# One count matrix less: a graph convolution that reads four typed planes in place of their sum

## The chip, the core and the metric

The kernel runs on one core of a Trainium2 chip. TensorE multiplies, VectorE (DVE) and ScalarE (ACT) do elementwise work, GpSimd (POOL) does elementwise work and indirect transfers, SyncE (SP) issues the other transfers. The metric is the device time of one execution in microseconds (us); lower is better. The kernel before took 18697.45 us, the median of three runs (18695.46 to 18709.6).

## The reference, cut to what matters

Four graph layers over 6250 nodes of 64 features and 206250 edges sorted by destination: attention, a graph convolution, message passing with two small networks, and four steps of a gated graph network. Two of them sum neighbours in a way that depends on the edge only through its two ends and its type:

```python
# layer 2, the convolution: the type of an edge plays no part
h = feat * norm[:, None]
agg = jax.ops.segment_sum(h[src], dst, num_segments=n)
rst = (agg @ weight) * norm[:, None] + bias
...
# layer 4, four times: each edge type has its own weights
transformed = jnp.einsum('nd,khd->knh', feat, W) + b[:, None, :]
msgs = transformed[etypes, src]
a = jax.ops.segment_sum(msgs, dst, num_segments=num_nodes)
```

## The kernel before, in words

Nodes stand in 49 blocks (`NB`) of 128 partitions. Both sums above are dense products with a matrix of edge counts: a row for each source node, a column for each destination, the entry the number of edges. The kernel makes these matrices first, in DRAM, and streams them later in chunks.

**The build** (about 302 to 5313 us). Columns are made in pairs, 3248 of them (`VW`; two destinations each, the last 112 for overflow), over 4859 steps (`BSTEPS`). In a step DVE makes two one-hot tiles (`hots_of`, L1690 and L1691, 128x128 and 128x392 elements, f16) in a ring of 8; TensorE multiplies them into a PSUM bank (`count`, L1090) and clears one column of the next bank (L1092). 392 is 2 destinations by 4 types by 49 source blocks. Before every fourth step TensorE loads twelve table values into registers (`fours`). ACT moves finished banks to `stagebuf` (`evict`, L823). When 16 pairs, 32 destinations, are staged, that is one event, 203 in all (`NEV`). For each event:

- SP (`keep`) waits for the evictions, loads four table values, stores the two halves of the four typed planes (L608, 784 KB each) to `adj4`;
- POOL (`untyped`) adds the four planes of the event in three additions of 128x1568 f16 elements (L766, L767, L769) into `ubuf`, a ring of 3;
- SP waits for the sum (`untyped_made`) and stores it to `adj1` (L612, 448 KB). Only then, and once the stores of the event before have landed (L615), does it count that event before as done (`events_done`, L616). ACT waits for this count before it reuses a stage buffer. Of these there are four, and two for the last seven events, which hold the overflow columns (`OBUFS`).

When all stores have landed, SP raises `built` and DVE starts the attention layer (L1697).

**The convolution** (about 8697 to 8948 us). The 6250 destinations are cut in 13 groups: one of 128 columns with 224 overflow columns (352 together), and twelve of 512. The 49 source blocks of `adj1` come in four chunks (`UCH`) of 14 blocks, of which the fourth is half empty: 52 transfers through a ring of four (`DRING`). For each source block TensorE makes two products with the same count columns: one with the first two bf16 parts of the features (L1176, 128 rows of output) and one with the third (L1181, 64 rows, left and right half of the array in turn). After a group come the overflow's share (`conv_fold`), the copy to SBUF by ACT and the product with the layer's weights (`conv_post`).

**The last layer**, four times, does the same with `adj4`: 196 blocks of a group in 14 chunks (L1373, L1378), and a product with the weights after each type.

All orders are written out by hand, one instruction stream per engine; a wait is on a semaphore.

Of the kernel before, what the change touches and what calls it, by code (L numbers as in the profile page):

```python
# [6 lines left out]
P = 128  # L7
N = 6250
D = 64
# [8 lines left out]
KT = 4  # L18
# [45 lines left out]
UCH = 4  # L64
# [5 lines left out]
ULEN = UCH * RUN  # L70
USED = NB * BLK
UBUFS = 3
# [9 lines left out]
ROWS1 = P * UCH * GRP  # L82
# [5 lines left out]
USED0 = NGRP * UCH  # L88
LOADED0 = 16 * USED0 // DRING
# [4 lines left out]
assert BW % GRP == 0 and COMBS % CCH == 0 and BC % 2 == 0 and NB <= UCH * CCH and (NGRP - 1) * 512 + P == NPAD  # L94
# [53 lines left out]
def build(nc, a, out):  # L148
    ctx = ExitStack()
    with ctx:  # L150
# [6 lines left out]
        def dram(name, shape, dt=F32):  # L157
            return nc.dram_tensor(name, shape, dt).ap()
# [10 lines left out]
        event_rows = dram("event_rows", (8, P), I32)  # L169
        adj4 = [dram(f"adj4_{h}", (NGRP * ROWS4 + GRP, RUN), F16) for h in range(2)]  # L170
        adj1 = dram("adj1", (NGRP * ROWS1 + GRP, RUN), F16)
# [72 lines left out]
        ubuf = here("ubuf", [P, UBUFS, ULEN], F16)  # L244
        uhalf = here("uhalf", [P, USED], F16)
# [117 lines left out]
        halves_made, untyped_made = sem("halves_made"), sem("untyped_made")  # L363
# [172 lines left out]
        def _(sp):  # L536
# [58 lines left out]
            table(2, event_rows, 4, eventtab)  # L595
            sp.wait_ge(tab_loaded, 16 * 10)

            def keep(k, j, it):
                last = sp.value_load(eventtab[0:1, k:k + 1] if known(k) else eventtab[0:1, bass.ds(k, 1)], min_val=1, max_val=1 << 14)
                src = sp.value_load(eventtab[32:33, k:k + 1] if known(k) else eventtab[32:33, bass.ds(k, 1)],  # L600
                                    min_val=0, max_val=(SBUFS + OBUFS - 1) * SLEN)
                row4 = sp.value_load(eventtab[64:65, k:k + 1] if known(k) else eventtab[64:65, bass.ds(k, 1)],
                                     min_val=0, max_val=(NGRP - 1) * ROWS4 + GRP - 1)
                row1 = sp.value_load(eventtab[96:97, k:k + 1] if known(k) else eventtab[96:97, bass.ds(k, 1)],
                                     min_val=0, max_val=(NGRP - 1) * ROWS1 + GRP - 1)
                sp.wait_ge(evicted, last)
                for h in range(2):
                    sp.dma_start(adj4[h][bass.ds(row4, ROWS4), :].rearrange("(p c k) e -> p c k e", p=P, k=GRP)[:, :, 0, :],  # L608
                                 stagebuf[:, bass.ds(src, SLEN)].rearrange("p (h c e) -> p h c e", h=2, e=RUN)[:, h, :, :])\
                        .then_inc(stored[j % 2], 16)  # L610
                sp.wait_ge(untyped_made, k + 1)
                sp.dma_start(adj1[bass.ds(row1, ROWS1), :].rearrange("(p c k) e -> p c k e", p=P, k=GRP)[:, :, 0, :],  # L612
                             ubuf[:, j % UBUFS, :].rearrange("p (c e) -> p c e", e=RUN)).then_inc(stored[j % 2], 16)
                if not (known(k) and k < 1):
                    sp.wait_ge(stored[(j - 1) % 2], (it * 3 + (j - 1) // 2 + 1) * 48)  # L615
                    sp.sem_inc(events_done, 1)  # L616
            pipeline(sp, NEV, 6, 0, lambda it, j: stage(NEV, 6, it, j, 0, keep))
            sp.wait_ge(stored[(NEV - 1) % 2], ((NEV - 1) // 2 + 1) * 48)
# [9 lines left out]
            for i in range(NGRP * UCH):  # L628
                n, c = divmod(i, UCH)
                width = GRP if n else GCOLS // BLK  # L630
                if i >= DRING:
                    sp.wait_ge(used, i - DRING + 1)
                sp.dma_start(chunk1[:, i % DRING, 0:width * RUN],
                             adj1[0:NGRP * ROWS1, :].rearrange("(g p c k) e -> g p c (k e)", p=P, c=UCH, k=GRP)[ORDER[n], :, c, 0:width * RUN])\
                    .then_inc(loaded[i % DRING], 16)
# [35 lines left out]
            with sp.Fori(0, LAYERS) as layer:  # L671
                for i in range(GCH):
                    n, c = divmod(i, NCH)
                    width = GRP if n else GCOLS // BLK
                    sp.wait_ge(used, layer * GCH + (max(i - DRING + 1, 0) + USED0))
                    sp.dma_start(chunk4[:, i % DRING, 0:width * RUN],
                                 adj4[c // HCH][0:NGRP * ROWS4, :].rearrange("(g p c k) e -> g p c (k e)", p=P, c=HCH, k=GRP)
                                 [ORDER[n], :, c % HCH, 0:width * RUN])\
                        .then_inc(loaded[i % DRING], 16)
                    if c == 6:  # L680
                        cols = 512 if n else P
                        sp.dma_start(counts[:, n % 2, 0:cols], count_rows[:, ORDER[n] * 512:ORDER[n] * 512 + cols])\
                            .then_inc(count_in[n % 2], 16)
# [8 lines left out]
        def _(pool):  # L692
# [59 lines left out]
            pool.wait_ge(tab_loaded, 16 * 10)  # L752

            def untyped(k, j, it):
                last = pool.value_load(eventtab[0:1, k:k + 1] if known(k) else eventtab[0:1, bass.ds(k, 1)],
                                       min_val=1, max_val=1 << 14)
                src = pool.value_load(eventtab[32:33, k:k + 1] if known(k) else eventtab[32:33, bass.ds(k, 1)],
                                      min_val=0, max_val=(SBUFS + OBUFS - 1) * SLEN)
                pool.wait_ge(evicted, last)
                if not (known(k) and k < UBUFS):  # L760
                    pool.wait_ge(events_done, k - UBUFS + 1 + EPRE)
                if not (known(k) and k < 1):
                    pool.wait_ge(untyped_made, k)
                kinds = stagebuf[:, bass.ds(src, SLEN)].rearrange("p (t e) -> p t e", t=KT)
                to = ubuf[:, j % UBUFS, 0:USED]
                nc.gpsimd.tensor_tensor(to, kinds[:, 0, :], kinds[:, 1, :], ALU.add).then_inc(halves_made, 1)  # L766
                nc.gpsimd.tensor_tensor(uhalf[:, :], kinds[:, 2, :], kinds[:, 3, :], ALU.add).then_inc(halves_made, 1)  # L767
                pool.wait_ge(halves_made, k * 2 + 2)
                nc.gpsimd.tensor_tensor(to, to, uhalf[:, :], ALU.add).then_inc(untyped_made, 1)  # L769
            pipeline(pool, NEV, UBUFS, 0, lambda it, j: stage(NEV, UBUFS, it, j, 0, untyped))  # L770


# [21 lines left out]
        def _(act):  # L794
# [11 lines left out]
            act.wait_ge(tab_loaded, 16 * 10)  # L806
# [54 lines left out]
            act.wait_ge(used, UCH)  # L861
# [67 lines left out]
            with act.Fori(0, LAYERS) as layer:  # L929
                gb, sb4 = layer * NGRP, layer * (NGRP * KT)  # L930

                def sweep(n, k):
                    i = n * KT + k
                    act.wait_ge(used, layer * GCH + (n * NCH + (3, 6, 10, 13)[k] + 1 + USED0))
                    if i >= 2:
                        act.wait_ge(posted, sb4 + NGRP + i - 1)
                    cols = 512 if n else GCOLS
                    nc.scalar.activation(summed4[:, k % 2, 0:cols], bank[k % 2][:, 0:cols], ACT.Copy).then_inc(copied, 1)
# [48 lines left out]
        def _(pe):  # L987
# [71 lines left out]
            turn_table(2, 8)  # L1059
# [13 lines left out]
            pe.wait_ge(tab_loaded, 16 * 10)  # L1073
# [92 lines left out]
            for n in range(NGRP):  # L1166
                cols = 512 if n else GCOLS
                for c in range(UCH):
                    i = n * UCH + c
# [3 lines left out]
                    combs = min(CCH, NB - c * CCH)  # L1173
                    for m in range(combs):
                        hi = c * CCH + m
                        nc.tensor.matmul(bank[n % 2][:, 0:cols], feat1[:, hi, 0:2, :].rearrange("p a d -> p (a d)"),  # L1176
                                         columns(chunk1, i % DRING, m, cols), start=hi == 0, stop=False, skip_group_check=True)
                    for m in range(combs):
                        hi = c * CCH + m
                        half = hi % 2 * D  # L1180
                        last = nc.tensor.matmul(bank[n % 2][half:half + D, 0:cols], feat1[:, hi, 2, :],  # L1181
                                                columns(chunk1, i % DRING, m, cols), start=False, stop=False, skip_group_check=True)
# [124 lines left out]
            with pe.Fori(0, LAYERS) as layer:  # L1307
# [55 lines left out]
                for n in range(NGRP):  # L1363
                    cols = 512 if n else GCOLS
                    for c in range(NCH):
                        i = n * NCH + c
                        times = GCH // DRING + (i % DRING < GCH % DRING)
                        pe.wait_ge(loaded[i % DRING], layer * (16 * times) + (16 * (i // DRING + 1) + LOADED0))
# [52 lines left out]
        def _(v):  # L1421
# [243 lines left out]
            link(both_(out=tabcols[:, 4:6], in0=i2[:, E2], scalar=float(ROWS4), in1=i3[:, E2], op0=ALU.mult, op1=ALU.add))  # L1665
            both_(out=tabcols[:, 6:8], in0=i2[:, E2], scalar=float(ROWS1), in1=i3[:, E2], op0=ALU.mult, op1=ALU.add)\
# [6 lines left out]
            copy_(tabi[0:8, :], bank[7][0:8, 0:P]).then_inc(tab_copied, 1)  # L1673
# [11 lines left out]
            link(nc.vector.memset(ubuf[:, :, USED:ULEN], 0.0))  # L1685
# [406 lines left out]
```

## Time and profile before

| | us |
|---|---|
| median of 3 runs | 18697.45 |
| the profiled execution | 18688.54 |
| its span, first to last instruction | 18686.8 |
| build of the count matrices | 302 to 5313 |
| convolution's products | 8702 to 8948 |

The span is what the trace covers; the execution's own time is 1.7 us more. In the rows below, PE is TensorE's matmuls and PEld its weight loads, which overlap them. Times are us from the start of the span. Behind an arrow in brackets stands what ended an idle time, "issue" being time in which the engine waited for nothing that the profile shows. PEclk is the granted TensorE clock as a share of 2.4 GHz; it takes the values 0.5 (1.2 GHz) and 1.0 (2.4 GHz), and a mean over a stretch lies between them.

### The profile page before, as it was taken

How to read it: one execution, taken by the hardware profiler on the slowest of the kernel's cores; microseconds unless marked ns; L12 is line 12 of the kernel's file. 1: busy time of each engine (PE TensorE's matmuls, PEld its weight loads, DVE VectorE, ACT ScalarE, POOL GpSimd, SP SyncE). 2: the span in 40 equal slices, each digit the busy share in tenths (PEclk: the TensorE clock that was granted, in tenths of full speed). 3: DMA queues.
4: the chain of work that ended last, by engine and by line, in shares of the span. 5: the costliest groups of instructions: out<-in, count | busy, mean ns of one | idle time of the engine just before them, and what ended most of it. 6: DMA issues, size and time to landing. Idle time of an engine off the chain costs nothing.

```text
span 18686.8 us, 316361 instructions
## 1 busy us (share of the span) xinstructions
PE 12122.4 (65%) x67022; PEld 7612.2 (41%) x67023; DVE 7552.7 (40%) x26048; ACT 3559.3 (19%) x9727; POOL 8136.1 (44%) x6693
## 2 busy tenths in 40 slices
PE   3444444444435555556777777677776899999999
PEld 2222222222234444444555555555555544444443
DVE  6777777777743333333333333333333200000000
ACT  1333333333310000000122222222222100000000
POOL 3333333333345555551588888888887000000000
PEclk6555555555555555556899999999999699999999
DMA  2222222222221111114333333333334598989898
GB/s 100 84 84 84 82 82 85 83 84 84 84 60 35 35 35 35 35 35 164 79 41 41 41 41 41 42 41 41 41 41 38 157 342 334 341 331 342 328 345 311
DMA packets 1285108, 2208.14 MB, mean 118 GB/s; under 512 B 407567, under 2 KB 1127717, under 8 KB 1183861
## 3 DMA queue, kind: packets, MB, share of 16 engines
q1 hardware_dynamic: 935388, 1916.06, 29.3%
q0 software_dynamic: 348960, 284.02, 11.5%
q14 instruction: 536, 4.39, 0.1%
q8 instruction: 224, 3.67, 0.1%
HBM read 1647.55 MB, written 551.99 MB: 118 GB/s over the span
## 4 chain that ended last, share of the span: by engine, by line
PE 30%; issue 20%; POOL 13%; another core or an unknown queue 4%; DVE 2%; DMA 1%; DVEq 0%; SPq 0%; POOLq 0%; ACT 0%; ACTq 0%
PE ps L1373 12%; POOL G L469 7%; PE ps L1378 6%; POOL reverse L788 5%; PE ps L1128 3%; PE ps L1118 2%; PE ps L1108 1%; PE ps L1315 1%; POOL scatter_hold L787 1%; DMA reverse<-SD,sidx 1%; PE ps L1176 1%; PE ps L1181 0%; PE ps L1331 0%; PE ps L413 0%
## 5 line engine op out<-in xcount | busy, mean ns | idle before, releaser
L1090 PE MATMUL ps<-hots 128*128 128x392 f16 x4859 | 2210.5, 505 | 2779.9 <-issue 1348.8
L788 POOL DMA_INDIRECT reverse<-SD,sidx x1660 | 2649.2, 1596 | 389.4 <-issue 378.3
L1691 DVE TENSOR_SCALAR hots<-count_hi,key_hi 128x392 f16<-128x392 f16 x4859 | 2682.9, 552 | 0.0
L1373 PE MATMUL ps<-chunk,feat 128*128 128x512 f16 (+1 forms) x10192 | 2278.9, 375 | 14.6 <-DVE feat L2002 13.5
L823 ACT ACTIVATE stagebuf<-ps 128x392 f32 x3248 | 1531.5, 502 | 3468.4 <-PE ps L1092 2408.6
L1690 DVE TENSOR_SCALAR hots<-count_lo,key_lo 128x128 f16<-128x128 f16 x4859 | 1620.0, 333 | 1343.9 <-PE ps L1092 1343.8
L1090 PEld LDWEIGHTS ps<-hots 128*128 128x128 f16 x4859 | 505.6, 104 | 3905.0 <-issue 3904.4
L766 POOL TENSOR_TENSOR ubuf<-stagebuf 128x1568 f16 x203 | 638.3, 3144 | 3086.3 <-ACT stagebuf L823 3086.3
L469 POOL DMA_INDIRECT G<-h_table,idx x1660 | 1658.9, 999 | 493.1 <-issue 486.4
L469 POOL DMA_INDIRECT G<-kv_table,idx x1660 | 1596.3, 962 | 518.4 <-issue 518.4
L1859 DVE TENSOR_TENSOR acc<-acc,ps 128x132 f32 x1660 | 485.4, 292 | 3087.1 <-PE ps L1239 2997.5
L1236 PE MATMUL ps<-MS,OH 128*128 128x128 f32 x3320 | 780.4, 319 | 1277.4 <-issue 745.8
L1373 PEld LDWEIGHTS ps<-chunk,feat 128*128 128x128 bf16 x10192 | 942.9, 98 | 1343.1 <-issue 349.4
L1962 DVE SCALAR_TENSOR_TENSOR gate_t<-ps,W,gate_rz 64x512 f32<-64x512 f32 (+1 forms) x52 | 37.1, 713 | 3228.1 <-ACT gate_rz L954 3228.1
L1236 PEld LDWEIGHTS ps<-MS,OH 128*128 128x128 f32 x3320 | 553.9, 200 | 1829.1 <-issue 1802.0
L1225 PE MATMUL ps<-W,OT 128*128 128x256 f32 x3320 | 1097.3, 414 | 246.1 <-issue 220.9
L1378 PE MATMUL ps<-chunk,feat 128*64 128x512 f16 (+1 forms) x10192 | 1213.7, 378 | 0.0
L885 ACT ACTIVATE SD<-ps 128x129 f32<-128x129 f32 x1660 | 463.2, 279 | 3825.0 <-DMA reverse<-SD,sidx 3816.7
L1128 PE MATMUL ps<-MS,OH 128*128 128x66 f32 x3320 | 811.2, 426 | 551.5 <-DVE acc L527 541.4
L1226 PE MATMUL ps<-big,OT 128*128 x3320 | 1058.3, 402 | 0.0
L1092 PE MATMUL ps<-zero 128*128 128x1 bf16 x4859 | 1023.2, 211 | 0.0
L1128 PEld LDWEIGHTS ps<-MS,OH 128*128 128x128 f32 x3320 | 739.2, 328 | 660.0 <-DVE acc L527 335.0
(392 smaller groups left out, 18370.2 us busy)
## 6 DMA issues: line engine op xcount, KB each, us to landing
chunk<-adj SPq DMA_DIRECT2D x720, 1792.0 KB, 8.9
adj<-stagebuf SPq DMA_DIRECT2D x406, 784.0 KB, 5.0
adj<-ubuf SPq DMA_DIRECT2D x203, 448.0 KB, 3.1
chunk<-adj SPq DMA_DIRECT2D x60, 1232.0 KB, 6.2
G<-in_edge SPq DMA_DIRECT2D x1660, 32.0 KB
G<-kv_table,idx POOLq DMA_INDIRECT x1660
G<-h_table,idx POOLq DMA_INDIRECT x1660
reverse<-SD,sidx POOLq DMA_INDIRECT x1660
```

The source lines that it names most:

```text
L469: nc.gpsimd.indirect_dma_start(G[:, j, 0:width], None, table, bass.IndirectOffsetOnAxis(idx[:, j:j + 1], 0))\
L788: nc.gpsimd.indirect_dma_start(reverse[j % R], bass.IndirectOffsetOnAxis(sidx[:, j:j + 1], 0), SD[:, j % R, :], None, compute_op=ALU.add). ...
L823: nc.scalar.activation(stagebuf[:, bass.ds(held["to"][j % 4], SLEN)].rearrange("p (x c) -> p x c", c=BLK)[:, :, 0:2], bank[j][:, 0:2 * COM ...
L1090: nc.tensor.matmul(ps[:, bass.ds(held["to"][j % 4], 2 * COMBS)], hots[:, j, 0:P], hots[:, j, P:P + 2 * COMBS], start=False, stop=True, ski ...
L1128: last = nc.tensor.matmul(bank[4 + j % 2][:, n * AC:(n + 1) * AC], OH[:, (j * GR + n) % HOT, :], messages[:, j % 2, n, :], start=True, sto ...
L1225: nc.tensor.matmul(bank[2 + j % 2][:, 0:2 * M], OT[:, j % 2, 0:P], w("edge"), start=True, stop=False)
L1226: nc.tensor.matmul(bank[2 + j % 2][:, 0:2 * M], OT[:, j % 2, P:2 * P], big[:, bass.ds(b * 2 * M, 2 * M)], start=False, stop=True).then_inc ...
L1236: nc.tensor.matmul(bank[6][:, 0:M], OH[:, j % HOT, :], MS[:, j % MR, 0:M], start=True, stop=True)
L1373: nc.tensor.matmul(bank[k % 2][:, 0:cols], feat[0][:, hi, 0:2, :].rearrange("p a d -> p (a d)"), columns(chunk4, i % DRING, m, cols), star ...
L1378: last = nc.tensor.matmul(bank[k % 2][half:half + D, 0:cols], feat[0][:, hi, 2, :], columns(chunk4, i % DRING, m, cols), start=False, stop ...
L1690: nc.vector.tensor_scalar(hots[:, j, 0:P], count_lo[:, :], part(key_lo[:, :], k, 1), None, ALU.is_equal)
L1691: nc.vector.tensor_scalar(hots[:, j, P:P + 2 * COMBS], count_hi[:, :], part(key_hi[:, :], k, 1), None, ALU.is_equal).then_inc(hot_made, 1)
```

## The change

`adj1`, `ubuf`, the three additions on POOL and their stores are taken out, with the fourth row of the event table. The convolution now reads the 14 chunks of `adj4` for each group, 182 transfers in place of 52, and multiplies all 196 blocks, the features of source block `b` once for each type, into the same PSUM bank. The rest of each group is as before. The counters of the ring that both layers share are adjusted.

```diff
-            table(2, event_rows, 4, eventtab)
-            sp.wait_ge(tab_loaded, 16 * 10)
+            table(2, event_rows, 3, eventtab)
+            sp.wait_ge(tab_loaded, 16 * 9)
...
                 sp.wait_ge(evicted, last)
                 for h in range(2):
                     sp.dma_start(adj4[h][bass.ds(row4, ROWS4), :].rearrange("(p c k) e -> p c k e", p=P, k=GRP)[:, :, 0, :],
...
-                sp.wait_ge(untyped_made, k + 1)
-                sp.dma_start(adj1[bass.ds(row1, ROWS1), :].rearrange("(p c k) e -> p c k e", p=P, k=GRP)[:, :, 0, :],
-                             ubuf[:, j % UBUFS, :].rearrange("p (c e) -> p c e", e=RUN)).then_inc(stored[j % 2], 16)
                 if not (known(k) and k < 1):
-                    sp.wait_ge(stored[(j - 1) % 2], (it * 3 + (j - 1) // 2 + 1) * 48)
+                    sp.wait_ge(stored[(j - 1) % 2], (it * 3 + (j - 1) // 2 + 1) * 32)
                     sp.sem_inc(events_done, 1)
...
-            for i in range(NGRP * UCH):
-                n, c = divmod(i, UCH)
+            for i in range(GCH):
+                n, c = divmod(i, NCH)
...
                 sp.dma_start(chunk1[:, i % DRING, 0:width * RUN],
-                             adj1[0:NGRP * ROWS1, :].rearrange("(g p c k) e -> g p c (k e)", p=P, c=UCH, k=GRP)[ORDER[n], :, c, 0:width * RUN])\
+                             adj4[c // HCH][0:NGRP * ROWS4, :].rearrange("(g p c k) e -> g p c (k e)", p=P, c=HCH, k=GRP)
+                             [ORDER[n], :, c % HCH, 0:width * RUN])\
...
-            def untyped(k, j, it):
-                last = pool.value_load(eventtab[0:1, k:k + 1] if known(k) else eventtab[0:1, bass.ds(k, 1)],
...
-                nc.gpsimd.tensor_tensor(to, kinds[:, 0, :], kinds[:, 1, :], ALU.add).then_inc(halves_made, 1)
-                nc.gpsimd.tensor_tensor(uhalf[:, :], kinds[:, 2, :], kinds[:, 3, :], ALU.add).then_inc(halves_made, 1)
-                pool.wait_ge(halves_made, k * 2 + 2)
-                nc.gpsimd.tensor_tensor(to, to, uhalf[:, :], ALU.add).then_inc(untyped_made, 1)
...
-                for c in range(UCH):
-                    i = n * UCH + c
+                for c in range(NCH):
+                    i = n * NCH + c
...
-                    combs = min(CCH, NB - c * CCH)
-                    for m in range(combs):
-                        hi = c * CCH + m
+                    for m in range(CCH):
+                        hi = (c * CCH + m) % NB
                         nc.tensor.matmul(bank[n % 2][:, 0:cols], feat1[:, hi, 0:2, :].rearrange("p a d -> p (a d)"),
...
-            link(nc.vector.memset(ubuf[:, :, USED:ULEN], 0.0))
```

TensorE's stream at the end of the first group (352 columns) and the start of the second (512). In the names, `ps` is PSUM, `feat_conv` the split features, x13 a repeat count. Before:

```order
L1176 MATMUL ps<-chunk,feat_conv 128x352 [waits loaded2]
L1176 MATMUL ps<-chunk,feat_conv 128x352 x13
L1181 MATMUL ps<-chunk,feat_conv 64x352 x14
L1176 MATMUL ps<-chunk,feat_conv 128x352 [waits loaded3]
L1176 MATMUL ps<-chunk,feat_conv 128x352 x6
L1181 MATMUL ps<-chunk,feat_conv 64x352 x7
L1176 MATMUL ps<-chunk,feat_conv 128x512 [waits loaded0]
```

The same place in the changed kernel:

```order
L1140 MATMUL ps<-chunk,feat_conv 128x352 [waits loaded1]
L1140 MATMUL ps<-chunk,feat_conv 128x352 x13
L1146 MATMUL ps<-chunk,feat_conv 64x352 x14
L1140 MATMUL ps<-chunk,feat_conv 128x512 [waits loaded2]
```

The half chunk is gone: every chunk has 14 pairs, and a group has fourteen chunks where it had three and a half.

SP's stream for one event of the build's loop, before:

```order
L608 ISA [waits evicted]
L608 DMA adj_0<-stagebuf 896x1x448
L608 ISA
L608 DMA adj_1<-stagebuf 896x1x448
L612 ISA [waits untyped_made]
L612 DMA adj<-ubuf 512x1x448
L599 TENSOR_LOAD eventtab [waits stored0]
```

and in the changed kernel:

```order
L596 ISA [waits evicted]
L596 DMA adj_0<-stagebuf 896x1x448
L596 ISA
L596 DMA adj_1<-stagebuf 896x1x448
L589 TENSOR_LOAD eventtab [waits stored0]
```

Between the evictions of an event and the count of the event before it nothing is left on SP but its own two issues.

## Rows read from the trace of the kernel before

**Rows 1.** Stretches: start:end, us, busy us of each engine, PEclk, DMA share, GB/s
```profile
302.00:5296.00 4994.00, 2214.81 (x9718) 1010.84 (x9718) 3643.66 (x9711) 1529.39 (x3244) 1909.83 (x606) 0.50 0.25 84
5600.00:8550.00 2950.00, 1509.66 (x9199) 1373.92 (x9197) 935.34 (x3444) 273.18 (x766) 1488.49 (x1609) 0.50 0.16 35
8702.00:8948.10 246.10, 244.28 (x1452) 109.96 (x1452) 13.57 (x39) 7.80 (x14) 0.00 (x0) 0.99 0.93 373
14791.60:15758.90 967.30, 948.75 (x5410) 401.25 (x5411) 72.86 (x146) 59.12 (x95) 0.00 (x0) 1.00 0.89 338
```

**Rows 2.** Waits of the build: us in total, times, longest us
```profile
PE ps L1090 <- issue: 1348.8, 639, 3.8
...
PE ps L1090 <- DVE hots L1691: 1174.8, 526, 3.7
...
PE ps L1090 <- ACT stagebuf L823: 256.3, 98, 5.9
```

**Rows 3.** Timeline of one event on DVE and POOL: start us, us, engine
```profile
2505.10 3.20 DVE L1690 TENSOR_SCALAR hots<-count_lo,key_lo 128x128 f16<-128x128 f16 x1
2505.10 3.14 POOL L766 TENSOR_TENSOR ubuf<-stagebuf 128x1568 f16 x1 [14.40 <-ACT stagebuf L823]
...
2508.21 3.25 DVE L1691 TENSOR_SCALAR hots<-count_hi,key_hi 128x392 f16<-128x392 f16 x1
...
2511.55 3.21 DVE L1691 TENSOR_SCALAR hots<-count_hi,key_hi 128x392 f16<-128x392 f16 x1
```

**Rows 4.** The build's two DVE lines: ns of one, min/median/max, first and last start
```profile
L1690 DVE TENSOR_SCALAR hots<-count_lo,key_lo x4859: 235/253/3237, 300.4 to 5289.0; 128x128 f16<-128x128 f16 x195
L1691 DVE TENSOR_SCALAR hots<-count_hi,key_hi x4859: 302/315/3258, 300.6 to 5289.2; 128x392 f16<-128x392 f16 x195
```

**Rows 5.** Timeline of PE between two events, first matmul of each four steps
```profile
2515.49 0.51 PE L1090 MATMUL ps<-hots 128*128 128x392 f16 x1 [1.78 <-DVE hots L1691]
...
2519.49 0.51 PE L1090 MATMUL ps<-hots 128*128 128x392 f16 x1 [2.18 <-DVE hots L1691]
...
2523.08 0.51 PE L1090 MATMUL ps<-hots 128*128 128x392 f16 x1 [1.78 <-issue]
```

**Rows 6.** L1090 alone, whole build and its last seven events: PE and PEld (count)
```profile
302.00:5296.00 4994.00, 2210.45 (x4859) 505.61 (x4859) 0.50 0.25 84
5140.00:5296.00 156.00, 51.63 (x113) 11.62 (x112) 0.50 0.28 93
```

**Rows 7.** Timeline of ACT in an overflow event
```profile
5242.68 1.67 ACT L823 ACTIVATE stagebuf<-ps 128x392 f32 x4 [10.83 <-SPq L616]
5246.22 1.67 ACT L823 ACTIVATE stagebuf<-ps 128x392 f32 x4 [1.88 <-issue]
```

**Rows 8.** Timeline of the build's end
```profile
5299.88 1.33 SPq L608 DMA_DIRECT2D adj<-stagebuf  x2
...
5312.90 0.70 DVE L1697 MEMSET S<- 128x768 f32 x1 [23.42 <-SPq L620]
```

**Rows 9.** DMA issues: xcount, KB each, us to landing
```profile
adj<-stagebuf SPq DMA_DIRECT2D x406, 784.0 KB, 5.0
```

**Rows 10.** Timeline of PE in the convolution, first matmuls of chunks
```profile
8707.23 2.26 PE L1176 MATMUL ps<-chunk,feat_conv 128*128 128x352 f16 x14
...
8710.59 2.26 PE L1176 MATMUL ps<-chunk,feat_conv 128*128 128x352 f16 x14
...
8721.52 3.18 PE L1176 MATMUL ps<-chunk,feat_conv 128*128 128x512 f16 x14
...
8726.27 3.19 PE L1176 MATMUL ps<-chunk,feat_conv 128*128 128x512 f16 x14
```

**Rows 11.** A stretch of the convolution, columns as in Rows 1
```profile
8720.00:8760.00 40.00, 40.00 (x244) 17.97 (x240) 3.97 (x12) 1.47 (x3) 0.00 (x0) 1.00 1.01 426
```

**Rows 12.** Timeline of DVE at the build's start, the ring still empty
```profile
300.41 0.25 DVE L1690 TENSOR_SCALAR hots<-count_lo,key_lo 128x128 f16<-128x128 f16 x1
...
300.81 0.25 DVE L1690 TENSOR_SCALAR hots<-count_lo,key_lo 128x128 f16<-128x128 f16 x1
```

More of the change, by code:

```diff
@@ L63 @@
 NCH = COMBS // CCH
-UCH = 4
 BLK = 32
@@ L69 @@
 RUN = CCH * BLK
-ULEN = UCH * RUN
-USED = NB * BLK
-UBUFS = 3
 GRP = 16
@@ L81 @@
 ROWS4 = P * HCH * GRP
-ROWS1 = P * UCH * GRP
 HALFC = BC // 2
@@ L87 @@
 DRING = 4
-USED0 = NGRP * UCH
-LOADED0 = 16 * USED0 // DRING
 CELL = 5
@@ L93 @@
 GCH = NGRP * NCH
-assert BW % GRP == 0 and COMBS % CCH == 0 and BC % 2 == 0 and NB <= UCH * CCH and (NGRP - 1) * 512 + P == NPAD
+ROUND = tuple(16 * (GCH // DRING + (q < GCH % DRING)) for q in range(DRING))
+assert BW % GRP == 0 and COMBS % CCH == 0 and BC % 2 == 0 and (NGRP - 1) * 512 + P == NPAD
 IDXQ = -(-CG // 4)
@@ L168, in build @@
         virt_rows = dram("virt_rows", (3 * VC, P), I32)
-        event_rows = dram("event_rows", (8, P), I32)
+        event_rows = dram("event_rows", (6, P), I32)
         adj4 = [dram(f"adj4_{h}", (NGRP * ROWS4 + GRP, RUN), F16) for h in range(2)]
-        adj1 = dram("adj1", (NGRP * ROWS1 + GRP, RUN), F16)
         count_rows = dram("count_rows", (KT, NGRP * 512))
@@ L243, in build @@
         stagebuf = here("stagebuf", [P, (SBUFS + OBUFS) * SLEN + BLK], F16)
-        ubuf = here("ubuf", [P, UBUFS, ULEN], F16)
-        uhalf = here("uhalf", [P, USED], F16)
         hots = here("hots", [P, BRING, P + 2 * COMBS], F16)
@@ L362, in build @@
         hot_made, step_done, evicted, events_done = (sem(n) for n in ("hot_made", "step_done", "evicted", "events_done"))
-        halves_made, untyped_made = sem("halves_made"), sem("untyped_made")
         stored = [sem(f"stored{q}") for q in range(2)]
@@ L603, in keep @@
                                      min_val=0, max_val=(NGRP - 1) * ROWS4 + GRP - 1)
-                row1 = sp.value_load(eventtab[96:97, k:k + 1] if known(k) else eventtab[96:97, bass.ds(k, 1)],
-                                     min_val=0, max_val=(NGRP - 1) * ROWS1 + GRP - 1)
                 sp.wait_ge(evicted, last)
@@ L610, in keep @@
                         .then_inc(stored[j % 2], 16)
-                sp.wait_ge(untyped_made, k + 1)
-                sp.dma_start(adj1[bass.ds(row1, ROWS1), :].rearrange("(p c k) e -> p c k e", p=P, k=GRP)[:, :, 0, :],
-                             ubuf[:, j % UBUFS, :].rearrange("p (c e) -> p c e", e=RUN)).then_inc(stored[j % 2], 16)
                 if not (known(k) and k < 1):
-                    sp.wait_ge(stored[(j - 1) % 2], (it * 3 + (j - 1) // 2 + 1) * 48)
+                    sp.wait_ge(stored[(j - 1) % 2], (it * 3 + (j - 1) // 2 + 1) * 32)
                     sp.sem_inc(events_done, 1)
             pipeline(sp, NEV, 6, 0, lambda it, j: stage(NEV, 6, it, j, 0, keep))
-            sp.wait_ge(stored[(NEV - 1) % 2], ((NEV - 1) // 2 + 1) * 48)
+            sp.wait_ge(stored[(NEV - 1) % 2], ((NEV - 1) // 2 + 1) * 32)
             sp.sem_inc(events_done, 1)
@@ L674, in _ @@
                     width = GRP if n else GCOLS // BLK
-                    sp.wait_ge(used, layer * GCH + (max(i - DRING + 1, 0) + USED0))
+                    sp.wait_ge(used, layer * GCH + (max(i - DRING + 1, 0) + GCH))
                     sp.dma_start(chunk4[:, i % DRING, 0:width * RUN],
@@ L750, in _ @@
                         .then_inc(key_gathered[h], 16)
-            pool.wait_ge(tab_loaded, 16 * 10)
-            def untyped(k, j, it):
-                last = pool.value_load(eventtab[0:1, k:k + 1] if known(k) else eventtab[0:1, bass.ds(k, 1)],
[L756 to L765, printed above, removed]
-                nc.gpsimd.tensor_tensor(to, kinds[:, 0, :], kinds[:, 1, :], ALU.add).then_inc(halves_made, 1)
-                nc.gpsimd.tensor_tensor(uhalf[:, :], kinds[:, 2, :], kinds[:, 3, :], ALU.add).then_inc(halves_made, 1)
-                pool.wait_ge(halves_made, k * 2 + 2)
-                nc.gpsimd.tensor_tensor(to, to, uhalf[:, :], ALU.add).then_inc(untyped_made, 1)
-            pipeline(pool, NEV, UBUFS, 0, lambda it, j: stage(NEV, UBUFS, it, j, 0, untyped))
             pool.wait_ge(table_stored, 16)
@@ L805, in _ @@
                 nc.scalar.activation(key_hi[:, lo:lo + n * P], bank[2 + q % 2][:, 0:n * P], ACT.Copy).then_inc(key_copied, 1)
-            act.wait_ge(tab_loaded, 16 * 10)
+            act.wait_ge(tab_loaded, 16 * 9)
             def fours(row, k, top):
@@ L859, in conv_copy @@
                 nc.scalar.activation(summed1[:, n % 2, 0:cols], bank[n % 2][:, 0:cols], ACT.Copy).then_inc(copied, 1)
-            act.wait_ge(used, UCH)
+            act.wait_ge(used, NCH)
             nc.scalar.activation(over1[:, :], bank[0][:, OVC:GCOLS], ACT.Copy).then_inc(over_copied, 1)
@@ L933, in sweep @@
                     i = n * KT + k
-                    act.wait_ge(used, layer * GCH + (n * NCH + (3, 6, 10, 13)[k] + 1 + USED0))
+                    act.wait_ge(used, layer * GCH + (n * NCH + (3, 6, 10, 13)[k] + 1 + GCH))
                     if i >= 2:
@@ L1058, in _ @@
             tally(bank[5][:, 0:1], nxt[:, 1, :], pair2[:, 0, 1:2], False).then_inc(answered, 1)
-            turn_table(2, 8)
+            turn_table(2, 6)
             for q in range(10):
@@ L1070, in _ @@
                 last.then_inc(key_turned, 1)
-            pe.wait_ge(tab_loaded, 16 * 10)
+            pe.wait_ge(tab_loaded, 16 * 9)
             pe.wait_ge(key_copied, 10)
@@ L1172, in _ @@
                         pe.wait_ge(copied, n - 1)
-                    combs = min(CCH, NB - c * CCH)
-                    for m in range(combs):
-                        hi = c * CCH + m
+                    for m in range(CCH):
+                        hi = (c * CCH + m) % NB
                         nc.tensor.matmul(bank[n % 2][:, 0:cols], feat1[:, hi, 0:2, :].rearrange("p a d -> p (a d)"),
[L1177 to L1180, printed above, removed]
+                                         columns(chunk1, i % DRING, m, cols), start=c == 0 and m == 0, stop=False,
+                                         skip_group_check=True)
+                    for m in range(CCH):
+                        hi = (c * CCH + m) % NB
+                        half = m % 2 * D
                         last = nc.tensor.matmul(bank[n % 2][half:half + D, 0:cols], feat1[:, hi, 2, :],
@@ L1366, in _ @@
                         i = n * NCH + c
-                        times = GCH // DRING + (i % DRING < GCH % DRING)
-                        pe.wait_ge(loaded[i % DRING], layer * (16 * times) + (16 * (i // DRING + 1) + LOADED0))
+                        times = ROUND[i % DRING]
+                        pe.wait_ge(loaded[i % DRING], layer * times + (16 * (i // DRING + 1) + times))
                         for m in range(CCH):
@@ L1664, in _ @@
             link(scalar_(tabcols[:, 2:4], f4[:, E2], float(SLEN), None, ALU.mult))
-            link(both_(out=tabcols[:, 4:6], in0=i2[:, E2], scalar=float(ROWS4), in1=i3[:, E2], op0=ALU.mult, op1=ALU.add))
-            both_(out=tabcols[:, 6:8], in0=i2[:, E2], scalar=float(ROWS1), in1=i3[:, E2], op0=ALU.mult, op1=ALU.add)\
+            both_(out=tabcols[:, 4:6], in0=i2[:, E2], scalar=float(ROWS4), in1=i3[:, E2], op0=ALU.mult, op1=ALU.add)\
                 .then_inc(tab_cols, 1)
@@ L1672, in _ @@
             v.wait_ge(tab_stored, 32)
-            copy_(tabi[0:8, :], bank[7][0:8, 0:P]).then_inc(tab_copied, 1)
+            copy_(tabi[0:6, :], bank[7][0:6, 0:P]).then_inc(tab_copied, 1)
             for c in range(BC):
```

## The prediction

> **What bounds the kernel now.** I read the page's slices first: they show stages that follow one another, so each part of the change is priced in its own stage. The busy time by stretch comes next [rows 1]. The build takes 4994 us, and in it no engine is full: PE 2215 us, DVE 3644, ACT 1529, POOL 1910. The convolution takes 246 us, and there PE is busy for 244 of them at a granted clock of 0.99. So the convolution is bound by TensorE, and the build needs a closer look.
>
> The waits of the build [rows 2] name TensorE's matmul L1090: it sits idle 1349 us for "issue", 1175 us behind DVE's one-hot tiles and 256 us behind ACT. The "issue" part is the table loads before every fourth step. The DVE part has a cause that the timeline of one event shows [rows 3]: the moment POOL begins an addition of 3.14 us, the DVE instruction that starts with it takes 3.20 us, and the next 3.25 us; a third is held beside the third addition. Their medians are 0.253 and 0.315 us [rows 4]. DVE is held for as long as POOL adds, some 9.4 us in each event. The ring of 8 tiles covers a part, then TensorE runs dry.
>
> The Trainium skill says in GPSIMD Engine Reference, Key points, that GpSimd shares its SBUF interfaces with VectorE and that DVE instructions in a two-port mode or with two SBUF inputs contend with it. The held instructions of this trace, 3.2 us for a median of 0.3, agree. Taken alone the rule speaks against my sum below: it would hand back all of DVE's held time; the second rival prices that.
>
> **The build, part by part.** What TensorE does when nothing holds DVE is seen between two events [rows 5]: eight steps from 2515.49 to 2523.08 us, 7.59 us, 0.949 us a step. It includes both table loads and no dry wait beyond them. DVE alone makes a step's tiles in 0.40 us [rows 12], and ACT empties four banks in 3.54 us [rows 7], 0.885 us for each of 3248 evictions, 2874 us in all. Both are well under TensorE's 4859 x 0.949 = 4610 us, so TensorE's own pace is next and becomes the bound. Today's 4994 us for 4859 steps is 1.028 us a step [rows 6].
>
> - Regular and overflow steps at TensorE's pace: 4994 - 4610 = 384 us less.
> - The last seven events are a case of their own: 113 steps in 156 us, 22.3 us an event. ACT stands still for 10.8 us in each [rows 7], since with two buffers it waits for SP, and SP for POOL's sum. Without the sum ACT needs 4 x 3.54 = 14.2 us for 16 evictions and then about 2 us until SP has issued its two stores (1.33 us, rows 8) and counted: 16.2 us an event, 113 us for seven, where TensorE's pace would allow 107. That takes 6 us off the gain: 378 us.
> - The end: the last typed store is issued at about 5300.5 us [rows 8] and needs 5.0 us to land [rows 9]; DVE could go on near 5306 instead of 5312.9. 7 us less.
> - A memset of `ubuf`, one table row and its register load, and 203 stores of 448 KB: no more than 1 us, since the transfers run at a share of 0.25 and nobody waits for them outside the overflow events. I count nothing.
>
> The build's gain is 378 + 7 = 385 us. Bounds: if the one stretch I read is 1% slower than the mean will be, 46 us more; if each of 203 events still cost TensorE one late bank of 0.3 us (one L1691), 61 us less. So 324 to 431. I take 385, the value of the clean stretch.
>
> **The convolution.** A chunk of 14 pairs takes 3.36 us at 352 columns (8707.23 to 8710.59) and 4.75 at 512 (8721.52 to 8726.27) [rows 10]. A group had 49 pairs, 3.5 chunks, and gets 196, 14 chunks: 10.5 more.
>
> - Twelve groups of 512: 12 x 10.5 x 4.75 = 598.5 us.
> - One group of 352: 10.5 x 3.36 = 35.3 us.
> - Fold, copy and weights' product of each group stay at their number. Nothing is beside these products that could hide them: DVE, ACT and POOL are idle, and the next layer needs the result.
>
> Sum: 634 us more. What could make it dearer is the supply. A chunk of 1792 KB (1.835 MB) in 4.75 us asks for 386 GB/s; the convolution has been fed at 426 GB/s for 40 us while the ring was refilled [rows 11], which is 4.31 us a chunk. The last layer reads the same `adj4`, by the same transfers, at 338 GB/s with TensorE busy for 949 of 967 us [rows 1], so there TensorE and not the supply sets the pace. I therefore price the transfers at nothing; at 338 GB/s they would cost 5.43 us a chunk, 12 x 14 x 0.68 = 114 us more, and 14 x (3.73 - 3.36) = 5 us in the first group. If on the other side the longer run of products lost its one cold start and its joints, 10 us less. So 624 to 753, and I take 634.
>
> **The sum.** -385 + 634 = +249 us. The profiled execution took 18688.5 us, so 18938 us for a like one. The median of the runs shown lies 9 us above it; half of that I add: 18942 us.
>
> **The rivals.**
>
> *The clock rises in the build (faster).* The build and the attention layer run at 0.50, 1.2 GHz, the convolution and the last layer at 2.4 GHz [rows 1]. With the stalls gone TensorE's busy share in the build goes from 2215/4994 = 0.44 to 2215/4610 = 0.48. If the chip then granted the upper level, the six short gaps of eight steps, about 0.43 us each, could shrink towards the 0.17 us that 393 columns take by 3.36 us for 14 pairs of 352 (0.24 us a pair of one full and one half-width product): at most 6 x 0.26 = 1.56 us in 7.59, 948 us; half of it, 474, gives 18464 us. It turns the result once it returns 249 us, that is from 0.898 us a step down. Against it: the attention layer has a busy share of 1510/2950 = 0.51 and stays at 0.50. Chance 0.04.
>
> The Trainium skill, TensorE: Matmul & The Clock Gate, Part 1, states that the slow level is the default and that activity releases it. This is what the rival leans on; the two stretches at 0.50 with shares of 0.44 and 0.51 speak against its coming true here.
>
> *DVE is the bound (faster).* Then all its held time would return: per step 0.253 + 0.315 = 0.568 us, 2760 us for 4859, in place of the 3644 us that DVE is busy in the build [rows 1, 4]: 884 us back, which gives 18688 + 634 - 884 = 18438 us. Against it: TensorE's 0.949 us a step with DVE free. Chance 0.02.
>
> *The gain stays out (slower still).* The waits behind DVE go, but another takes their place: ACT's banks or SP's count, as in the overflow events. Then only the end's 7 us come back: 18688 + 634 - 7 = 19315 us. For it: 256 us of waits behind ACT. Against it: these too fall mostly where POOL's sum holds SP. Chance 0.05.
>
> *The supply binds the convolution.* 18942 + 119 = 19061 us. For it: the DMA share of 1.01 in the first 40 us [rows 11]. Against: the last layer. Chance 0.09.
>
> **How the numbers follow.** The forecast case has 0.80 and a range of its own from 18890 to 19010, by the bounds of the two sums. The range to 19075 takes in the supply case; with 18875 below it about 0.88 is inside. A change of 0.2% (37 us) is about what a measurement of this kernel can tell. Faster by more than that: 0.04 + 0.02 = 0.06. Within it: 0.02, the far edge of the forecast's case. Slower: 0.92.
>
> **What would show it.** No DVE line above 0.35 us in the build and L1690 and L1691 near 0.25 and 0.32 in the mean; the build's matmuls over 4610 to 4640 us; waits of L1090 behind DVE near nothing, those for issue larger; ACT's waits for SP in the last seven events at some 2 us; the first DVE memset of the next stage within 7 us of the last store's issue; chunks of the convolution 4.75 us apart fourteen to a group, at a granted clock of 1.0. The prediction is wrong if the build's step stays above 0.97 us or falls under 0.93, or if TensorE waits for `chunk` in the convolution for more than 20 us.

## The result: slower, by twice what was forecast

The changed kernel takes 19204.52 us, the median of four runs, against 18696.46: 2.71% slower, 95% interval of the ratio 1.0255 to 1.0288. The forecast was 18942 us, in a range to 19075. The direction was right, the size was not.

The two profiled spans differ by 515.0 us. Cut at the first tile of each stage the trace says where they lie:

| stage | before | after | difference |
|---|---|---|---|
| build, first to last L1090 | 4992.6 | 4882.5 | -110 |
| from there to the next stage's first memset | 17.5 | 9.1 | -8 |
| convolution, first to last full-width product | 241.0 | 872.4 | +631 |
| all the rest | | | +2 |

The convolution's cost came as predicted (+634). The build gave 118 us with its end, where 385 were promised: that is the whole error. Of the build's 110 us, 41 come from its last 113 steps, the seven overflow events (155.5 us before, 114.7 after); all the steps before them gave 69.

The stretches of the changed kernel, build and convolution (columns as in [rows 1]):

```profile
302.00:5184.60 4882.60, 2210.54 (x9717) 1013.01 (x9717) 2182.06 (x9706) 1530.08 (x3245) 0.00 (x0) 0.50 0.20 66
...
8581.60:9458.00 876.40, 875.82 (x5266) 381.92 (x5266) 13.14 (x38) 7.74 (x14) 0.00 (x0) 1.00 0.95 371
```

DVE's busy time in the build fell from 3644 to 2182 us and POOL is gone, yet the build is only 110 us shorter. Its waits (those of before in [rows 2]):

```profile
PE ps L1055 <- issue: 2426.7, 1111, 3.9
...
PE ps L1055 <- ACT stagebuf L788: 243.9, 102, 3.4
ACT stagebuf L788 <- SPq L601: 32.9, 12, 2.8
PE ps L1055 <- DVE hots L1654: 3.1, 2, 1.8
```

Of the 1175 us behind DVE 3 are left. In their place "issue" has grown from 1349 to 2427 us. DVE's two lines are as fast as their medians promised (columns of the page's groups: busy us, mean ns):

```profile
L1653 DVE TENSOR_SCALAR hots<-count_lo,key_lo 128x128 f16<-128x128 f16 x4859 | 1236.8, 255 | 2694.7 <-PE ps L1057 2694.7
...
L1654 DVE TENSOR_SCALAR hots<-count_hi,key_hi 128x392 f16<-128x392 f16 x4859 | 1538.5, 317 | 0.0
```

What "issue" hides shows in the timeline around one event of the changed kernel:

```profile
2489.26 1.32 SPq L596 DMA_DIRECT2D adj<-stagebuf  x2
2490.57 0.51 PE L1055 MATMUL ps<-hots 128*128 128x392 f16 x1 [1.78 <-issue]
...
2495.89 0.50 PE L1055 MATMUL ps<-hots 128*128 128x392 f16 x1 [3.51 <-issue]
...
2499.50 0.51 PE L1055 MATMUL ps<-hots 128*128 128x392 f16 x1 [1.79 <-issue]
```

Four steps with their table loads take 3.6 us elsewhere, or 4.0 where the loop turns. Here, right behind the stores' issue, they take 5.3. The load instruction itself tells why. Its line in the kernel before, then in the changed one (ns, min/median/max):

```profile
L1079 PEldq TENSOR_LOAD <-steptab x3645: 332/504/1321, 301.1 to 5293.9; - x192
```

```profile
L1044 PEldq TENSOR_LOAD <-steptab x3645: 333/504/1187, 300.1 to 5183.1; - x192
```

Three such loads stand before every fourth step. In a clean stretch they take 0.51, 0.34 and 0.50 us, 1.34 together. I sorted the 3645 records by the time since SP had finished issuing the last typed store: in each of the first four microseconds their mean is 0.9 to 1.15 us, from the fifth on 0.4 to 0.65. Both kernels have it: 513 loads of over 0.7 us before, 468 after. In the kernel before, the event's stores and POOL's first addition begin within 0.15 us of one another (the addition at 2505.10 in the event of [rows 3]), so the slow loads and the hold of DVE lay on top of each other:

```profile
2504.95 1.34 SPq L608 DMA_DIRECT2D adj<-stagebuf  x2
```

The end of the build and the convolution's chunks, to be compared with [rows 8, 10]:

```profile
5193.69 0.70 DVE L1660 MEMSET S<- 128x768 f32 x1 [14.95 <-SPq L605]
```

```profile
8753.04 3.20 PE L1140 MATMUL ps<-chunk,feat_conv 128*128 128x512 f16 x14
...
8757.80 3.20 PE L1140 MATMUL ps<-chunk,feat_conv 128*128 128x512 f16 x14
```

A chunk takes 4.76 us, and in the whole convolution TensorE waits for `chunk` once, for 72 us, before the first product; the kernel before waits there too (74 us in three waits).

### The profile page after: what moved, and what is told of

Same layout as the page of the kernel before. It is cut to its first block, busy times and chain, and to the rows that moved or that the text cites. A ratio compares the mean times of both kernels' runs of the same rounds, so it can differ in the third digit from the quotient of the medians.

```text
span 19201.8 us, 319169 instructions
## 1 busy us (share of the span) xinstructions
PE 12765.8 (66%) x70844; PEld 7899.8 (41%) x70845; DVE 6083.0 (32%) x26046; ACT 3557.1 (19%) x9727; POOL 6222.0 (32%) x6083
## 4 chain that ended last, share of the span: by engine, by line
PE 40%; issue 29%; POOL 13%; DVE 6%; another core or an unknown queue 5%; ACTq 2%; ACT 2%; DVEq 1%; DMA 1%; SPq 0%; POOLq 0%
PE ps L1338 12%; POOL G L459 7%; PE ps L1343 6%; PE ps L1055 6%; POOL reverse L753 5%; DVE hots L1654 3%; PE ps L1140 3%; PE ps L1093 2%; ACT stagebuf L788 2%; PE ps L1146 2%; PE ps L1083 1%; ACTq L774 1%; PE ps L1073 1%; PE ps L1280 1%
## 5 line engine op out<-in xcount | busy, mean ns | idle before, releaser
L457 POOL TENSOR_TENSOR hold_out<-hold_in 128x1 f32<-128x1 f32 x166 | 78.4, 472 | 7079.7 <-DMA kv_table<-big 4987.7
L1653 DVE TENSOR_SCALAR hots<-count_lo,key_lo 128x128 f16<-128x128 f16 x4859 | 1236.8, 255 | 2694.7 <-PE ps L1057 2694.7
L1654 DVE TENSOR_SCALAR hots<-count_hi,key_hi 128x392 f16<-128x392 f16 x4859 | 1538.5, 317 | 0.0
```

The costliest lines, as they stand in the source:

```text
L1653: nc.vector.tensor_scalar(hots[:, j, 0:P], count_lo[:, :], part(key_lo[:, :], k, 1), None, ALU.is_equal)
L1654: nc.vector.tensor_scalar(hots[:, j, P:P + 2 * COMBS], count_hi[:, :], part(key_hi[:, :], k, 1), None, ALU.is_equal).then_inc(hot_made, 1)
```

## The experiments

Theory A: the typed stores slow TensorE's table loads while they read SBUF; that is what fills the build once DVE is free, and in the kernel before it lay under the hold of DVE. The rivals are named in the expectations. Each run's kernel is the kernel before or the changed kernel with the edit that its text names. "Build" is the first to the last matmul of the one-hot tiles, "last" the part of it that the last 113 steps (the seven overflow events) take, and "loads" the sum of the load instruction's durations, all read from the trace's records. The times come from several sets of runs, in which the kernel before took 18691 to 18708 us, and the stage between build and convolution, which no edit touches, took 3370 to 3411 us in these traces. So the build column is the sharper measure: conv4, whose build nobody touched, repeats it within 0.3 us.

| kernel | KB stored an event | POOL's additions | build us | last us | loads us | time us |
|---|---|---|---|---|---|---|
| before | 2016 | yes | 4992.6 | 155.5 | 1930 | 18696 |
| changed | 1568 | no | 4882.5 | 114.7 | 1910 | 19205 |
| pool_adds | 1568 | yes | 4963.2 | 148.5 | 1909 | 19304 |
| no_adds | 2016 | no | 5007.4 | 119.5 | 2035 | 18716 |
| half_store | 784 | no | 4672.8 | 105.5 | 1700 | 19005 |
| half_adds | 784 | yes | 4855.3 | 148.5 | 1704 | 19166 |
| double_store | 3136 | no | 5214.9 | 135.9 | 2236 | 19560 |
| dram_copy | 784, and 784 DRAM to DRAM | no | 4706.2 | 108.4 | 1734 | 19019 |
| split8 | 2016 | in 24 pieces | 4962.4 | 176.8 | 1929 | 18670 |
| eights | 2016 | yes | 4637.9 | 157.0 | 1716 | 18340 |
| split8_eights | 2016 | in 24 pieces | 4422.6 | 178.2 | 1683 | 18128 |
| after_eights | 1568 | no | 4351.0 | 110.2 | 1688 | 18656 |
| conv4 | 2016 | yes | 4992.9 | 155.6 | 1930 | 19322 |

**pool_adds**: the changed kernel with the additions back, and with them SP's wait for the sum before it counts an event.

```diff
+                sp.wait_ge(untyped_made, k + 1)
...
+                nc.gpsimd.tensor_tensor(to, kinds[:, 0, :], kinds[:, 1, :], ALU.add).then_inc(halves_made, 1)
+                nc.gpsimd.tensor_tensor(uhalf[:, :], kinds[:, 2, :], kinds[:, 3, :], ALU.add).then_inc(halves_made, 1)
+                pool.wait_ge(halves_made, k * 2 + 2)
+                nc.gpsimd.tensor_tensor(to, to, uhalf[:, :], ALU.add).then_inc(untyped_made, 1)
```

> The changed kernel with GpSimd's three additions for each event put back; nobody reads their result and nothing stores it. Theory A (DVE held by GpSimd and TensorE's table loads slowed by the typed stores happen in the same microseconds, so the additions cost only what sticks out): the build goes from 4883 us back to about 4990, the time from 19205 to about 19315 us. Rival B (GpSimd's hold was worth the 378 us of my sum and something new in the changed kernel, such as stores that start earlier, eats the rest): build 5260, time about 19580 us.

Measured: build +81 us to 4963, where 4990 were expected, time 19303.6 us (ratio to before 1.0318, 1.0301 to 1.0336). TensorE's waits in the build:

```profile
PE ps L1083 <- issue: 1344.6, 635, 4.1
...
PE ps L1083 <- DVE hots L1682: 1143.9, 524, 3.5
...
PE ps L1083 <- ACT stagebuf L816: 261.8, 104, 4.6
```

The list of the kernel before is back, 1144 us behind DVE among it, and all of it is worth 81 us. Theory A holds, and rival B's 378 is out. Of the 81 us, 34 lie in the last seven events, where ACT again stands still for 71 us until SP has the sum; only 47 are left for the hold of DVE in all the steps before.

**no_adds**: the kernel before without the additions, its three stores kept.

```diff
-                sp.wait_ge(untyped_made, k + 1)
...
-            pipeline(pool, NEV, UBUFS, 0, lambda it, j: stage(NEV, UBUFS, it, j, 0, untyped))
...
-            link(nc.vector.memset(ubuf[:, :, USED:ULEN], 0.0))
+            link(nc.vector.memset(ubuf[:, :, :], 0.0))
```

> The kernel before without GpSimd's three additions and SP's wait for them; the third store of each event (448 KB) stays, of zeros, so the convolution's sums are zero. Theory A, by which each 1568 KB of stores slow the loads by about 1.6 us an event: 448 KB more cost some 0.4 us x 203 = 90 us against the changed kernel's build, so the build is about 4970 us and the time about 18670, against 18696. Rival B: the build is near 4616 us, the time near 18310. Rival C (what is left in the build is ACT's banks, whatever is stored): build 4883 as in the changed kernel, time about 18580.

Measured: 18715.9 us, ratio 1.0003 (0.9994 to 1.0013): no change that the runs can tell. TensorE waits 3 us behind DVE and 2536 us for "issue". Its build is 125 us longer than the changed kernel's, as its loads are (2035 against 1910): the third store, now issued some 1.5 us behind the start of the first, lengthens the slow window. Theory A had put it at 90. Rivals B and C are out. Two things moved in this edit: the additions went, which pool_adds prices at 81 us, and the third store came forward from some 10 us behind the first, and its price grew. Together they win nothing.

**half_store, double_store**: the dose, half and twice the bytes that the changed kernel stores.

```diff
-                for h in range(2):
+                for h in range(1):
...
```

```diff
-                for h in range(2):
-                    sp.dma_start(adj4[h][bass.ds(row4, ROWS4), :]
+                for h in range(4):
+                    sp.dma_start((adj4 + copy4)[h][bass.ds(row4, ROWS4), :]
...
```

> The changed kernel storing only the first half of the typed planes (784 KB an event); the convolution and the last layer read that half twice, so their sums are others. Theory A: the slow window of TensorE's table loads halves, the excess of 321 us over its clean pace falls to about 160, build about 4720 us. Rival C (ACT's banks) and rival D (loads slowed by SP's own work or by the events as such): build stays within 30 us of 4883.

> The changed kernel storing the typed planes twice, the second time to tensors that nobody reads (3136 KB an event). Theory A: the slow window doubles, build about 5150 to 5250 us, time about 19500. Rivals C and D: build within 40 us of 4883.

Measured: builds of 4673 and 5215 us, 210 less and 332 more. The loads' time moved by 210 less and 326 more. So the build follows the loads nearly one to one, and these follow the bytes stored. The slow window does too: counted from an event's first issue, the loads average over 0.85 us in the 2nd and 3rd microsecond of half_store, in the 2nd to 5th of the changed kernel and in the 2nd to 10th of double_store. Rivals C and D are out.

**dram_copy**: half_store, and the other half's bytes moved from DRAM to DRAM.

```diff
+                sp.dma_start(side[bass.ds(row4, ROWS4), :].rearrange("(p c k) e -> p c k e", p=P, k=GRP)[:, :, 0, :],
+                             a["edge"][0:P * HCH * RUN // 2 // D, :].rearrange("r d -> (r d)")
+                             .rearrange("(p c e) -> p c e", p=P, c=HCH)).then_inc(stored[j % 2], 16)
```

> The changed kernel storing only the first half of the typed planes from SBUF (as in half_store, read twice by the convolution and the last layer), and beside it for each event a copy of the same size and pieces from DRAM to DRAM. If reading SBUF by DMA is what slows TensorE's table loads, the build is that of half_store, 4673 us; if any DMA traffic or SP's issue of it does, it is that of the changed kernel, 4883 us or more.

Measured: build 4706 us, 33 more than half_store, where the same bytes out of SBUF cost 210. The copy did run beside the loads; it was under way for longer than a typed store, which lands after 5.0 us:

```profile
side<-in_edge SPq DMA_DIRECT2D x203, 784.0 KB, 6.2
```

Most of the slowing comes with reading SBUF by DMA; some 16% came with traffic or issue alone.

**half_adds**: half_store with the additions.

> half_store with GpSimd's three additions put back, unread. With full stores the additions cost 4963 - 4883 = 80 us of build. Theory A: half of the slow loads' shadow is gone, so the same additions now cost more, 150 to 280 us: build 4820 to 4950. If their price does not depend on the stores it is 80 us again, build 4753.

Measured: build 4855 us. The same additions cost 183 us with half the stores and 81 with all of them; before the last seven events 139 against 47. The cheaper the loads, the dearer the hold: each hides behind the other.

**split8, eights, split8_eights**: two edits of the kernel before.

```diff
+                def pieces(o, x, y, done):
+                    for c in range(0, USED, 196):
+                        last = nc.gpsimd.tensor_tensor(o[:, c:c + 196], x[:, c:c + 196], y[:, c:c + 196], ALU.add)
+                    last.then_inc(done, 1)
...
```

```diff
-                    steptab[row:row + 1, k:k + 4] if known(k) else steptab[row:row + 1, bass.ds(k, 4)], engines=(pe.engine,),
+                    steptab[row:row + 1, k:k + 8] if known(k) else steptab[row:row + 1, bass.ds(k, 8)], engines=(pe.engine,),
...
-                if j % 4 == 0:
+                if j % 8 == 0:
```

> The kernel before with each of GpSimd's additions of 1568 elements cut into eight of 196 (24 short ones an event), so that DVE gets in between. Theory A (the hold of DVE lies in the shadow of the loads that the stores slow): DVE's wait disappears from TensorE's list, but the build stays at 4960 to 5010 us and the time within 40 us of before. Rival B (the hold was worth what my sum gave it): build near 4620, time near 18330.

> The kernel before with TensorE's table values loaded eight at a time instead of four, half the loads. Theory A says that TensorE's load time (1930 us in the kernel before) is the cost to attack: if a load of eight values costs what one of four does, some 950 us go; part of this is then caught by the hold of DVE, which no longer has the loads to hide behind. Build 4150 to 4450 us. Rival E (a load's time goes by its values): build stays within 60 us of 4993.

> Both edits together on the kernel before. Theory A: now that the loads are halved the hold of DVE is exposed, and cutting the additions gives back 100 us or more beyond the run with loads of eight alone: build 3950 to 4250 us, time 17650 to 17950. Rival: the two runs with loads of eight are within 30 us of each other.

split8 measured 18669.7 us, 0.9987 (0.9977 to 0.9996): 26 us less, as theory A has it. But one half of my expectation failed: DVE's wait did not disappear, it grew from 1175 to 1319 us. The timeline of split8 shows the pieces and DVE taking turns:

```profile
2501.77 3.15 POOL L768 TENSOR_TENSOR ubuf<-stagebuf 128x196 f16 x6
...
2502.80 0.66 DVE L1695 TENSOR_SCALAR hots<-count_hi,key_hi 128x392 f16<-128x392 f16 x1
2503.39 0.54 DVE L1694 TENSOR_SCALAR hots<-count_lo,key_lo 128x128 f16<-128x128 f16 x1
2503.85 0.66 DVE L1695 TENSOR_SCALAR hots<-count_hi,key_hi 128x392 f16<-128x392 f16 x1
```

A step's tiles now take 1.04 us during 12.6 us, where before three instructions were held for 9.4. In the steps before the last seven events this wins 52 us of build, about what pool_adds gives for the whole hold (47); in the last seven the later sum costs 21. So the hold's price is gone although its waits grew.

eights measured 18340.2 us (0.9811, 0.9795 to 0.9828), 355 us less. A load of eight values takes more than one of four, less than two (median 763 ns against 504):

```profile
L1079 PEldq TENSOR_LOAD <-steptab x1824: 592/763/2089, 298.6 to 4937.4; - x183
```

so the loads' sum fell by 214 us and not by 950, and the build by 355, well short of the forecast 540 to 840. The build's gain beyond 214 lies outside the records of the load. A group of three loads also brings register work: in the changed kernel, in a clean stretch, the weight loads at the head of four steps and at the next step, with the idle time before each in brackets, read:

```profile
2490.57 0.10 PEld L1055 LDWEIGHTS ps<-hots 128*128 128x128 f16 x1 [2.07 <-issue]
...
2490.99 0.10 PEld L1055 LDWEIGHTS ps<-hots 128*128 128x128 f16 x1 [0.20 <-issue]
```

The three loads are 1.34 of the 2.07 us, a step's own share is 0.20, and 0.5 us are left. 607 groups fewer make about 300 us by this estimate, 514 with the loads. Only 355 of them came, because the hold of DVE now stuck out: split8_eights gets most of the rest back.

With both edits the time is 18127.6 us, 0.9698 (0.9681 to 0.9714), the fastest of all. Cutting the additions gives 215 us of build on top of eights, against 30 alone (before the last seven events 236 against 52): once more the hold costs what the loads no longer cover. The time missed its range by 178 us, since the loads fell by less than expected.

**after_eights** and **conv4**: the longer loads on the changed kernel, and the convolution's half of the change alone (the loops and the source of its chunks as in the diff above, the sums kept).

> The changed kernel with loads of eight values. In the kernel before this edit gave 355 us, with the hold of DVE still there, and 570 with the additions cut. Without any additions it should give more: build 4250 to 4400 us, time 18570 to 18720, about that of the unchanged kernel before and some 500 us above the best version so far. If the load time is not what fills the build, less than 300 us.

> The kernel before with only the convolution's side of the change: it reads the four typed planes; the sums on GpSimd and their stores stay and nobody reads them. All theories: build as before (4993 us), convolution 872 us in place of 241, time 18697 + 631 = 19328 us. If the last layer or the message pass shared in the cost, it would be more.

after_eights: 18655.9 us, 0.9982 (0.9972 to 0.9991), build 4351 us: 531 us gained, more than the 355 of the kernel before, since nothing holds DVE. The loads (222 us) and the register work (about 300) account for it. Before the last seven events its build takes 4241 us and that of split8_eights 4244: cutting the additions frees TensorE of the hold about as fully as taking them out does. With the convolution's cost it ends 528 us above split8_eights. conv4: 19322.5 us, 1.0338 (1.0317 to 1.0359), build 4992.9 us, convolution 871.9: the convolution's part costs 632 us and touches nothing else.

## Why the prediction was off, step by step

- **What holds DVE**: right. The three lines of 3.2 us were POOL's, and they are gone.
- **The build at TensorE's pace, 384 us**: this is the step that failed. "TensorE's own pace" was read between two events, 7.59 us for eight steps, and multiplied by all 4859. That stretch was free of the hold of DVE, but just as free of slow loads: its six took 0.33 to 0.51 us. So the sum missed an overlap: the loads that the typed stores slow ran under the hold of DVE, and they stay. The term measured 110 us. The clean pace is right as a floor: 4610 us plus the loads' excess over 1215 x 1.34 = 1628 us gives 4892 for the changed kernel (measured 4883), 4682 for half_store (4673), 5218 for double_store (5215), 5017 for no_adds (5007), 4716 for dram_copy (4706). For the kernel before it gives 4912: of the 384 us 302 were slow loads, and only 81 were more.
- **Where the 110 us lie**: the sum had the last seven events fall from 156 to 113 us, and they fell to 114.7, so 41 us. That part, ACT's standstill for SP, was right. The steps before them were to give some 335 us and gave 69: 47 by the additions (pool_adds) and 22 by the third store and what waited for it.
- **The bound of 61 us for "one late bank"**: too narrow for the same reason. The only leftover I allowed for was one of DVE's instructions; the range therefore stopped 130 us short of the result.
- **The stores at nothing**: wrong in kind. I looked only at who waits for them; 203 more stores cost the loads 125 us in no_adds without anyone waiting. In the place that they had in the kernel before they cost less: the build is 29 us longer than that of pool_adds, its loads 21.
- **The end, 7 us less**: right, it gave 8. ACT's waits for SP in the build fell from 95 to 33 us in all, and in the last seven events from 76 us to none.
- **The convolution, +634**: right, 631. The transfers hid, the clock stayed at 1.00.
- **The rivals**: "the gain stays out" (19315 us) came nearer in size than the forecast, but with another mechanism: the waits behind DVE were replaced by TensorE's own loads and not by ACT's banks (244 us, 256 before), and not fully. The clock stayed at 0.50 through the build at a busy share of 0.45, DVE did not bind, and the supply did not bind the convolution. The prediction's own sign of being wrong came true: the build's step is 1.005 us, over its 0.97. In the trace before, the load's own line with its maximum of 1321 ns would have shown the second cause.

The Trainium skill states in GPSIMD Engine Reference, Key points, that GpSimd shares its SBUF interfaces with VectorE, and that DVE instructions in a two-port mode or with two SBUF inputs contend with it. The traces agree on the contention: with whole additions a one-hot instruction took up to 3.26 us, with pieces up to 0.70, and in the runs without additions never over 0.33 us. Which mode these instructions ran in no trace shows. The price of the additions was 81 us of build beside all the stores and 183 beside half of them.

## What to carry to other kernels

A wait's total in the profile is not what its removal returns: ask what else runs slowly in the same microseconds, and read the floor in a stretch that has every other burden on it, not in the quietest one. Price a stage's special cases (here seven events out of 203, 41 of 110 us) apart from the rest. Where an engine's idle time reads "issue", look at its sequencer's own lines, register loads first, with their minimum, median and maximum. Four times the products made the convolution 3.6 times as long here (872 us against 241), since nothing stood beside it; such an exchange pays only if the stage that is relieved is bound by what was taken away.

## What the runs showed of the hardware

- A register load of four values from SBUF by TensorE's sequencer took 0.33 to 0.51 us, one of eight 0.59 to 0.76; for some four microseconds after SP has issued 1568 KB of stores out of SBUF the four-value load takes 0.9 to 1.15 us in the mean.
- 784 KB more from SBUF cost the build 210 us over 203 events, the same bytes from DRAM to DRAM 33 us. Which part of the path they share was not tried.
- A DVE tensor-scalar of f16 tiles that meets a GpSimd addition waits for the whole instruction, 3.2 us; against pieces of 0.55 us it alternates, 0.54 and 0.66 us for 0.25 and 0.32.
